# Feed-forward: the floor of the inner rows' largest values, made on GpSimd instead of on VectorE

## The reference

```
def _act_quant(x):
    scale = 127.0 / jnp.clip(jnp.max(jnp.abs(x), axis=-1, keepdims=True), 1e-05)
    xq = jnp.clip(jnp.round(x * scale), -128.0, 127.0) / scale
    ...
def _bitlinear(x, w):
    return jnp.einsum('bsi,oi->bso', _act_quant(x), _weight_quant(w))
...
gate = jax.nn.silu(_bitlinear(x, w_gate))      # 256 -> 1024
up = _bitlinear(x, w_up)
return _bitlinear(gate * up, w_down)           # 1024 -> 256
```

## Time and profile before

| | |
|---|---|
| median of three runs | 714.04 us (713.55 to 714.66) |
| span of the profiled execution, first to last instruction | 712.5 us |
| the profiled execution's time outside its span | not listed; the median is 1.54 us above the span |
| PE busy | 672.1 us (94%) |
| DVE busy | 633.6 us (89%) |
| ACT busy | 374.0 us (52%) |
| POOL busy | 353.7 us (50%) |
| granted TensorE clock, mean | 0.992 |

### The profile page before, as it was taken

How to read it: one execution, slowest core, us unless ns; L and a number is a source line. 1 busy time by engine, 2 the same in 40 slices (tenths; PEclk the granted TensorE clock), 3 DMA queues, 4 the chain that set the end, 5 groups by cost and what they waited for, 6 DMA issues and landing times. The chain is left out here.

```text
span 712.5 us, 12566 instructions
## 1 busy us (share of the span) xinstructions
PE 672.1 (94%) x4412; PEld 491.7 (69%) x4412; DVE 633.6 (89%) x1259; ACT 374.0 (52%) x722; POOL 353.7 (50%) x491
## 2 busy tenths in 40 slices
PE   9889999999989998899999799799999999999995
PEld 3478765887747886468886586567877776666664
DVE  4998787999989999989999979748999996999997
ACT  4732157031255503463232633669777776888885
POOL 0633424646135762158451571391692224788785
PEclk9999999999999999999999999999999999999998
DMA  8630045232522436143663065730000000000012
GB/s 311 180 61 1 0 119 104 74 60 25 64 51 38 104 133 60 29 89 60 192 104 74 0 197 88 256 100 2 2 3 2 2 2 1 1 31 31 32 60 90
DMA packets 35353, 50.51 MB, mean 71 GB/s; under 512 B 4857, under 2 KB 29433, under 8 KB 35035
## 3 DMA queue, kind: packets, MB, share of 16 engines
q0 software_dynamic: 7680, 16.77, 15.1%
q1 hardware_dynamic: 26746, 32.15, 13.9%
q10 hardware_dynamic: 864, 0.79, 0.4%
HBM read 29.79 MB, written 7.34 MB: 52 GB/s over the span
## 5 line engine op out<-in xcount | busy, mean ns | idle before, releaser
L744 ACT ACTIVATE yb<-banks 128x256 f32<-128x256 f32 x64 | 24.2, 386 | 149.2 <-PE banks L445 104.1
L470 PE MATMUL banks<-xt_in,w_in 128*128 128x512 f32 x192 | 87.9, 611 | 0.2
L436 PE MATMUL banks<-inv_m,spec_y 128*128 128x256 f32 x384 | 85.5, 379 | 0.0
L390 PE MATMUL banks<-z_cplx,fwd_m 128*128 128x256 f32 x240 | 72.2, 382 | 9.7 <-DVE prod L1130 5.4
L436 PEld LDWEIGHTS banks<-inv_m,spec_y 128*128 128x128 f32 x384 | 73.0, 190 | 9.9
L391 PE MATMUL banks<-z_cplx,fwd_m 128*128 128x256 f32 x240 | 71.4, 379 | 0.0
L470 PEld LDWEIGHTS banks<-xt_in,w_in 128*128 128x128 f32 x192 | 36.7, 194 | 43.3 <-issue 39.8
L390 PEld LDWEIGHTS banks<-z_cplx,fwd_m 128*128 128x128 f32 x240 | 44.8, 190 | 19.0 <-issue 8.4
L391 PEld LDWEIGHTS banks<-z_cplx,fwd_m 128*128 128x128 f32 x240 | 45.6, 190 | 6.2
L1816 ACT ACTIVATE silu<-ps_score,gate_back 128x1024 f32<-128x1024 f32 x32 | 35.6, 1114 | 19.0 <-issue 17.5
L1786 ACT ACTIVATE prob_t<-ps_pt 128x1024 f32<-128x1024 f32 x32 | 32.7, 1022 | 24.1 <-PE ps_pt L1591 24.1
(11 more groups left out here) (299 smaller groups left out, 1726.7 us busy)
## 6 DMA issues: line engine op xcount, KB each, us to landing
x_tok<-in_x SPq DMA_DIRECT2D x8, 512.0 KB, 4.2
x_tok<-in_b_out POOLq DMA_DIRECT2D x8, 512.0 KB, 13.7
v_t<-left POOLq DMA_DIRECT2D x8, 511.5 KB, 4.5
x_t<-left POOLq DMA_DIRECT2D x8, 511.5 KB, 5.3
xt_in<-in_x_t SPq DMA_DIRECT2D x3, 1024.0 KB, 5.9
x_scratch<-x_tok SPq DMA_DIRECT2D x6, 512.0 KB, 4.0
x<-x_scratch SPq DMA_DIRECT2D x6, 512.0 KB, 9.3
out<-x SPq DMA_DIRECT2D x6, 512.0 KB, 2.9
```

The source lines that it names most:

```text
L390: mm(o, fwd_m[:, at + 2 * half + odd, :], zz[:, 0, :], start=True, stop=False)
L436: last = mm(bank[:, odd * 2 * P:(odd + 1) * 2 * P], spec_y[:, j + odd, part * D + h * P:part * D + (h + 1) * P], inv_m[:, o:o + 2 * P], st ...
L470: last = mm(proj_pair(b, t)[:, c * 512:(c + 1) * 512], w_in[:, k, TILES[t] * P:(TILES[t] + 1) * P], xt_in[:, k, c * 512:(c + 1) * 512], st ...
```

## The change

The function floor_peak moves from VectorE's list to GpSimd's. The instruction is the same (a tensor_scalar, the larger of h_peak and CLIP, times 1/127, 128 x 1). On GpSimd it stands first in the slot, ahead of round_x(s + 3), and waits for the reduction of that slot (h_peaked). VectorE's hidden_scale waits for it (h_floored) as before; the reduction gets a wait for the floor of four tiles ago, since it overwrites what that one read.

```diff
@@ GpSimd
+            def floor_peak(i):
+                pool.wait_ge(h_peaked, i + 1)
+                if i >= CH:
+                    pool.wait_ge(h_scaled, i - CH + 1)
+                k = i % CH
+                ts(h_unit[:, k:k + 1], h_peak[:, k:k + 1], CLIP, 1.0 / QMAX, ALU.max, ALU.mult).then_inc(h_floored, 1)
...
             for s in range(TILES_ALL):
+                floor_peak(s)
                 if s + 3 in tiles:
                     round_x(s + 3)
                 back_hidden(s)
@@ VectorE
                 dve.wait_ge(h_ready, i + 1)
+                if i >= CH:
+                    dve.wait_ge(h_floored, i - CH + 1)
                 reduce(h_peak[:, k:k + 1], hid[:, k, :], AX_X, ALU.max, apply_absolute_value=True)\
                     .then_inc(h_peaked, 1)
-
-            def floor_peak(i):
-                dve.wait_ge(h_peaked, i + 1)
-                if i >= CH:
-                    dve.wait_ge(back_down, i - CH + 1)
-                k = i % CH
-                ts(h_unit[:, k:k + 1], h_peak[:, k:k + 1], CLIP, 1.0 / QMAX, ALU.max, ALU.mult).then_inc(h_floored, 1)
...
-                floor_peak(s)
                 hidden_scale(s)
...
             hidden(LAST)
-            floor_peak(LAST)
             hidden_scale(LAST)
```

## The result

The changed kernel takes 721.33 us (median of four runs, 721.10 to 721.43), beside 713.79 for the kernel before (four runs, 713.46 to 714.66). The ratio is 1.0098, with a 95% interval of 1.0085 to 1.0111: slower by 7.5 us. The forecast was 719.0 with a range of 716.6 to 721.7. The profiled execution took 721.1 us, 1.8 us more than its span.

The account below looks back on a forecast made before the run. VectorE was taken as the bound by a small margin; stalls less slot gains +5.0, ends +0.3, slot 22 -0.34 made +5.0 on the 712.5 us span, 717.5, plus 1.54 to the median: 719.0, range 716.6 to 721.7.

Parts of the forecast that it names:

- own range: Whole kernel: 717.6 to 720.2 us, the span of the main forecast, which had 80 in 100.
- rival C: Handover at the upper price: ordinary slots gain nothing, stalls nearly as long, +7.6, 721.6 us; 10 in 100.
- uneven slots: GpSimd's slots 4, 8, 12, ... 28, with norm or output factors; the following slots' stalls sum to 8.63 us.
- Rival A: GpSimd is free in time, so no stalls come in the feed-forward: -3.7, 710.4 us; 5 in 100.
- rival B: Stalls half as long, 0.6 instead of 1.23 each: +0.6, 714.6 us, no measurable change; 5 in 100.
- 4.40 us until floor(13) can start: GpSimd's queue from floor(12): 0.16, round_x 0.445, down_back 0.16, then 3.64; VectorE stands still for 1.315 us.
- The gain of an ordinary slot is 0.185 - 0.055 = 0.13: VectorE's ordinary slots: removed floor saves 0.185 us, scale starts 0.055 late through the handover; 3.51 over 27 slots.
- The sum of the stretch: Feed-forward slots: stalls of 8.63 us, less 3.62 gained in the slots and 0.34 in slot 22.
- It catches up each time: GpSimd in the feed-forward, busy 81%, about 87% with 0.19 us more per slot: its lateness doesn't pile up.
- The ends: Slots 0 to 2 gain nothing; slots 3 and 31 pay +0.15 us each for the handover, +0.3 together.
- So -0.34: Slot 22's x_unit, 0.51 us where its like took 0.17, no longer collides with GpSimd's xq_f on the shared port.
- What is queued behind the new wait ... is in time: GpSimd's round_x, down_back and inner-row rounding stand behind the floor's wait; their delay was to cost nothing.

Follow-up runs that it names:

- ten: Changed kernel with the power in the output factors of the first six chunks replaced by a product: 715.83 us, ratio 1.0022.
- Experiment six: Changed kernel without the two added buffer-guarding waits (GpSimd's for h_scale, VectorE's for h_unit, each of four tiles ago): 721.93 us, ratio 1.0111.
- experiment two: Kernel before, its floor kept on VectorE, plus an idle copy of the floor on GpSimd that nobody waits for: 714.63 us, ratio 1.0008.
- Four: Changed kernel with the floors of slots 5, 9, ... 29 back on VectorE: 716.43 us, ratio 1.0035.
- five: Changed kernel with VectorE making h_scale of slots 5, 9, ... 29 behind the next slot's inner rows: 718.83 us, ratio 1.0071.
- seven: Changed kernel with GpSimd making each chunk's shift and first normalization one slot later: 717.36 us, ratio 1.0042.
- Experiment eight: Changed kernel with the floor on GpSimd only in slots 4 to 30 with s mod 4 of 0 or 3, otherwise VectorE: 712.65 us, ratio 0.9976.
- nine: Changed kernel with h_scale taken from h_peak (clip and factor 127 left out) and round_x ahead of the floor on GpSimd: 714.99 us, ratio 1.0009.
- three: Changed kernel with h_scale taken from h_peak, not the floor (clip and factor 127 left out), floors staying on GpSimd: 712.98 us, ratio 0.9984.
- one: Changed kernel with GpSimd's floor behind round_x in its slot instead of ahead of it: 722.02 us, ratio 1.0111.

## Why the prediction was right, and where its sizes were off

**The range: right by its width.** The direction and the place of the loss were right. The time, 721.33, lies outside the forecast's "own range" of 717.6 to 720.2. It lies in the range given only because that was widened to take in rival C, whose mechanism did not happen. The change cost 7.5 us where 5.0 had been forecast.

**The bound and the mechanism: right.** "VectorE is the bound by a small margin, and anything that it waits for in these slots moves the end." The stalls came in slots 5, 9, 13, 17, 21, 25 and 29, behind the uneven slots, and ten showed their cause. Four of them, of 1.58 to 1.62, are longer than the 1.1 to 1.4 that the text had named. Rival A (GpSimd free in time) and rival B (stalls half as long) are refuted by the 10.9 us of waits. Rival C gave 721.6, as close to the measured 721.33 as a forecast could be, but for another reason: it wanted ordinary slots without a gain, and they gained more than forecast. Its number hit, its mechanism didn't happen. The test the prediction had named for it, "a gap in every slot", failed.

**"4.40 us until floor(13) can start": the step that was mis-sized.** It measured 4.69 (641.36 to 646.05). The sum took the floor as a 128x1 instruction like down_back, with 0.16 to the next start, and let it begin where round_x had begun. The floor takes 0.21 to 0.25 and round_x starts 0.30 or more after it; and it starts 0.63 after the normalization, where round_x had started 0.525 after it. That is 0.14 and 0.10 too little, and the remainder of 0.05 lies in the factors' own starts. The stall of slot 13 follows: 1.315 forecast, 1.59 measured. (For slot 9 the text has GpSimd 0.53 later than in slot 12; the rows give 4.19 - 3.64 = 0.55, which changes little.) The bounds of the prediction covered the floor's duration ("above, a floor of 0.22"), but not the time around it. Over the seven stalled slots the loss against before was 9.5 us, where 7.7 had been forecast (8.63 less seven times 0.13).

**"The gain of an ordinary slot is 0.185 - 0.055 = 0.13": too small.** It was 0.17. The way back was the reason: the floor ended at 641.57 and the scale started at 641.61, so 0.04 instead of the 0.10 read in another stage. Eighteen ordinary slots without another effect gave 3.0 us, 0.6 more than forecast. The lower end of the prediction's bounds, 0.05, was the nearer value.

**The sum of the stretch.** Forecast: 8.63 - 3.62 - 0.34 = 4.67. Measured: 6.18. The difference of 1.5 is 1.8 more in the stalled slots, 0.6 less in the ordinary ones, and 0.3 in slot 20, where VectorE stood still for 0.36 us ahead of w_raw(21). That gap is no cost of its own. Experiment six doesn't have it; its stall in slot 21 is 1.58 where this one is 1.23, and its stretch is the same, 96.52. So what the sum had missed in the stalls is 2.1 us rather than 1.8.

**"It catches up each time": true of the trace, misleading as a reason.** GpSimd does wait for VectorE again in slot 14, by 0.37. But the 87% was a sum of busy times. Taken start to start, its list from floor to floor is 4.69, 2.98, 2.64 and 2.64 us, 12.95 per chunk, against VectorE's 12.9 without stalls in the four slots from 12 (13.56 before, less four times 0.17). From slot 23 on there is no x_peak, and four slots of VectorE would take four times 3.05, 12.2: there GpSimd's list is the longer one. At VectorE's old pace, in experiment two, GpSimd caught up once in every chunk, by 0.3 to 0.7 us; at the new pace it caught up because VectorE stood still. Four, five and seven showed the consequence: a stall healed in one place comes back in the next slot. The text's 0.19 per floor was too low: each floor takes 0.30 of GpSimd's queue, and another 0.10 ahead of it where it waits for nothing.

**The ends: right.** Slot 3 +0.11 and the tail +0.12, forecast +0.15 each; what slots 1 and 2 gained was lost at slot 3.

**"So -0.34" in slot 22: right.** Its x_unit took 0.17, at 678.38, and the slot fell from 3.83 to 3.32. Experiment eight has no stalls; there the instruction meets one of GpSimd's that began before it. It is long again, and ends when GpSimd's normalization does, 671.92 + 0.46 = 672.38 beside 671.82 + 0.54 = 672.36:

```profile
671.92 0.46 DVE L2140 TENSOR_SCALAR x_unit<-x_peak 128x4 f32<-128x4 f32 x1
...
671.82 0.54 POOL L2028 TENSOR_SCALAR x<-x,f_rstd,f_shift 128x256 f32<-128x256 f32 x1
```

The second row is GpSimd's, from the same kernel's timeline. The Trainium skill (SBUF — State Buffer, "Who interferes with whom") has the loser of the shared port pair blocked for the other's whole instruction; both rows agree with it. So do four and nine (0.46 and 0.66, each ending 0.02 after GpSimd's instruction); where x_unit began before a wide instruction of GpSimd's, it took 0.16 to 0.18. But the rule is not the whole of it. In slot 9 of the change x_unit began and ended while GpSimd's power was running, and wasn't held up:

```profile
629.65 1.03 POOL L2016 TENSOR_TENSOR f_rstd<-f_rstd,a_half_neg 128x4 f32<-128x4 f32 x1
...
630.03 0.17 DVE L2138 TENSOR_SCALAR x_unit<-x_peak 128x4 f32<-128x4 f32 x1
```

Nor were the floors, not even beside wide instructions. In the kernel before, three of them began while a GpSimd tensor_scalar was running and took 0.15 all the same, in slots 6, 10 and 26. The first:

```profile
618.73 0.47 POOL L1976 TENSOR_SCALAR xq_f<-x,x_scale 128x256 f32<-128x256 f32 x1
...
618.85 0.15 DVE L2154 TENSOR_SCALAR h_unit<-h_peak 128x1 f32<-128x1 f32 x1
```

So it was right to give their blocking nothing. Why x_unit is held up beside a 128x256 or 128x1024 instruction and not beside the power, and why a floor isn't held up at all, no run here shows.

**"What is queued behind the new wait ... is in time": right.** In slot 13 the matrix engine waited 0.83 us for round_x, and then 0.48 for VectorE:

```profile
646.91 0.29 PE L1642 MATMUL ps_pt<-f_ident,xq_f 128*128 128x128 bf16 x2 [0.83 <-POOL xq_f L1976]
...
648.13 1.02 PE L1651 MATMUL ps_score<-w_up,xq_t 128*128 128x512 bf16 x4 [0.48 <-DVE w_raw L2149]
```

So it was early all the same. This held only because VectorE stalled too: in three, where it didn't stall at h_scale, the lateness of round_x reached it and ate 2.4 us. So taking the stalls away would not have been enough for rival A's 710.4: three had none, with a larger gain per slot, and was only 1.1 us faster than its kernel before.

**The distance from span to median.** "1.54 above that span; I keep the distance": it was 2.0 after. Together with the 0.53 us of the stage ahead it makes 1.0 of the 2.3 us by which the forecast was short. Neither has to do with the change: over all the kernels run, w_raw(0) began anywhere from 593.3 to 595.4.

## What to carry to other kernels

Before work is moved from the bound engine to another, lay the two queues side by side slot by slot, start to start, and ask when the other engine gets to the moved instruction in its worst slot, not how busy it is on average. A result on which the bound engine waits must be made where the helper's queue is short; where the helper's work is uneven, move the instruction only in the slots that have room (experiment eight: two slots in four gave -1.6 us, all of them +7.5). And count the occupancy of small instructions from start to start: 0.21 us of busy time took 0.30 to 0.40 of the queue.

## What the runs showed of the hardware that was not expected

- A 128x1 tensor_scalar on GpSimd takes 0.21 to 0.25 us, a 128x1 tensor_tensor 0.19; the next start comes 0.30 to 0.34 after the one and mostly 0.16 after the other. The tile's rows:

```profile
L1989 POOL TENSOR_SCALAR h_unit<-h_peak x32: 212/213/249, 597.0 to 709.4; 128x1 f32<-128x1 f32 x32
...
L1996 POOL TENSOR_TENSOR down_back<-h_unit,w_mean x32: 188/192/194, 597.8 to 709.7; 128x1 f32<-128x1 f32 x32
```

- A waiting VectorE began 0.03 us after the end of GpSimd's small instruction (646.05 + 0.23 to 646.31), against 0.10 behind one of 0.72 us.
- Idle time without a cause in the profile: ahead of w_raw(21) VectorE stands still for 0.36 us (the "issue" line above; 670.43 + 0.16 to 670.96). It is there in the change and in experiments one, three, five, seven, nine and ten (0.36 to 0.42), and absent before and in two, six and eight. Four has one of 0.38 ahead of w_raw(31) and one of 0.26 ahead of the floor of slot 9. Where a stall follows, as in the change, one and ten, that stall is shorter by as much (in ten 0.38, where its like in slot 13 has 0.73), and the gap costs nothing. In six the two waits were gone, in two and eight VectorE kept nearly its old rhythm; what it is stays open.
